# Layer norm applied behind the down projection, with the bounds, the last latents and the weight loads reordered

## The reference

```python
def _layernorm(x):
    return (x - mean(x)) / sqrt(var(x) + 1e-5)

def attn(x):                       # x is the normalised input
    C_q = x @ Wq_d + bq_d          # 1024 -> 12
    C_kv = x @ Wkv_d + bkv_d       # 1024 -> 4
    q = (C_q @ W_qk + b_qk).reshape(b, s, 32, 4)
    attn = softmax(einsum('bqhd,bkd->bhqk', q, C_kv) / sqrt(4))
    V = (C_kv @ Wv_u + bv_u).reshape(b, s, 32, 32)
    return einsum('bhqk,bkhd->bqhd', attn, V).reshape(b, s, 1024) @ Wo + bo

x = x + attn(_layernorm(x))
x = x + ffn(_layernorm(x))         # x @ W.T + bias + sum of eight LoRA products
```

## Time and profile before

| | us |
|---|---|
| three runs | 2119.95, 2121.74, 2122.32 |
| median | 2121.74 |
| the profiled execution | 2122.61 |
| its span, first to last instruction | 2120.8 |
| ACT busy in the span | 1993.5 |
| PE busy in the span | 1958.8 |
| DVE / POOL busy in the span | 504.6 / 180.0 |
| mean granted clock of TensorE | 0.989 |

### The profile page before, as it was taken

One profiled execution on the slowest core, in us unless ns is written; L12 is line 12 of the kernel. 1 busy time (PEld: TensorE's weight loads), 2 busy tenths in 40 slices (PEclk: granted clock), 3 DMA queues, 4 the chain that ended last, 5 costly groups with the idle time before them and its releaser, 6 DMA issues. The chain is left out here.

```text
span 2120.8 us, 35990 instructions
## 1 busy us (share of the span) xinstructions
PE 1958.8 (92%) x15023; PEld 710.0 (33%) x15023; DVE 504.6 (24%) x1307; ACT 1993.5 (94%) x2193; POOL 180.0 (8%) x100
## 2 busy tenths in 40 slices
PE   4757899899999999999999999999999999999999
PEld 3411222233333333333333333333333333333337
DVE  8732343212111111212111111212111111212115
ACT  6968999999999999999999999999999999999970
POOL 1210001000010001100010001100020001100021
PEclk8989999999999999999999999999999999999999
DMA  7541201000010000100010000100010000100010
GB/s 240 184 122 38 84 13 35 5 15 20 18 45 6 25 13 25 35 15 15 24 45 5 25 13 25 35 15 13 25 45 5 22 16 25 35 15 13 25 40 40
DMA packets 45661, 77.42 MB, mean 37 GB/s; under 512 B 15870, under 2 KB 29750, under 8 KB 45498
## 3 DMA queue, kind: packets, MB, share of 16 engines
q1 hardware_dynamic: 45498, 75.11, 10.8%
HBM read 51.23 MB, written 23.86 MB: 35 GB/s over the span
## 5 line engine op out<-in xcount | busy, mean ns | idle before, releaser
L573 ACT ACTIVATE probs<-ps 128x1024 f32<-128x1024 f32 x2048 | 1900.1, 1030 | 34.3 <-PE ps L783 23.8
L794 PE MATMUL ps<-probs,c_wide 128*32 128x512 f32 x8192 | 989.8, 601 | 0.0
L783 PE MATMUL ps<-q_in,key_t 27*128 27x512 bf16 x4096 | 405.1, 386 | 102.9 <-ACT probs L573 91.4
L840 PE MATMUL ps<-w_eff,xn_t 128*128 128x512 f32 x1344 | 394.6, 418 | 0.0
L794 PEld LDWEIGHTS ps<-probs,c_wide 128*32 128x32 f32 x8192 | 212.7, 108 | 426.6 <-issue 221.6
L783 PEld LDWEIGHTS ps<-q_in,key_t 27*128 27x128 bf16 x4096 | 103.0, 91 | 734.7 <-ACT probs L573 714.9
L1263 DVE SCALAR_TENSOR_TENSOR y<-ps,nw,y 128x512 f32<-128x512 f32 x64 | 48.0, 751 | 977.5 <-PE ps L840 967.7
L840 PEld LDWEIGHTS ps<-w_eff,xn_t 128*128 128x128 f32 x1344 | 228.2, 188 | 102.2 <-issue 69.8
L481 POOL TENSOR_TENSOR y<-y,ffn_bias 128x1024 f32<-128x1024 f32 x32 | 76.4, 2387 | 1355.3 <-DVEq L1284 1355.3
L476 POOL TENSOR_TENSOR y<-y,attn_bias 128x1024 f32<-128x1024 f32 x32 | 75.5, 2381 | 481.2 <-DMA y<-in_L_attn_x_dram 481.0
L1247 DVE TENSOR_TENSOR y<-ps,y 128x512 f32<-128x512 f32 x64 | 44.2, 690 | 137.5 <-PE ps L817 137.1
(11 more groups left out here) (136 smaller groups left out, 593.8 us busy)
## 6 DMA issues: line engine op xcount, KB each, us to landing
y<-in_L_attn_x_dram SPq DMA_DIRECT2D x48, 512.0 KB, 4.2
out_dram<-y SPq DMA_DIRECT2D x32, 512.0 KB, 2.7
area<-in_L_attn_x_dram SPq DMA_DIRECT2D x16, 512.0 KB, 4.9
q_in<-q_parts SPq DMA_DIRECT2D x256, 27.0 KB
q_parts<-q_parts_sb SPq DMA_DIRECT2D x48, 128.0 KB, 2.2
y<-in_L_attn_Wo_dram SPq DMA_DIRECT2D x1, 2048.0 KB, 8.5
xn<-in_L_attn_Wo_dram SPq DMA_DIRECT2D x1, 2048.0 KB, 13.5
y<-in_L_ffn_W_dram SPq DMA_DIRECT2D x1, 2048.0 KB, 7.7
```

What stands on the lines that cost most here:

```text
L573: nc.scalar.activation(probs[:, (c * STEPS + step) % PROBS, bass.ts(pair, 2 * N)], ps[:, 2 * (i % SCORE_SLOTS):2 * (i % SCORE_SLOTS) + 2, ...
L783: last = nc.tensor.matmul(ps[:, at, :], key_t[TILE * h:TILE * h + KEYS, bass.ts(b * KT + kt, P)], q_in[TILE * h:TILE * h + KEYS, g % 2, :] ...
L794: last = nc.tensor.matmul(ps[32 * h:32 * h + 32, SUMS, :], c_wide[:, b * KT + kt, at:at + 32], probs[:, (c * STEPS + step) % PROBS, bass.t ...
L840: last = nc.tensor.matmul(ps[:, SHARED, :], xn_t[:, t % 2, a, kb, :], w_eff[:, b, kb, bass.ts(half, N)], start=(kb + i == 0), stop=(kb == ...
```

## The change

The first layer norm is no longer applied to x. PE transposes x as it is loaded. From w_down its column mean is taken off (PE sums the columns with a product with ones, DVE subtracts w_mean), so that the mean of a row drops out, and 1/sqrt of the variance is applied to the down projection: POOL finds it from x_mv (deviations_x, 14 instructions on 128x4), writes it on the diagonal of four 128x128 blocks (diag), PE spreads it over all partitions with a product with ones (spread_r, bank 5), ACT moves that into o_sb (move_r), and DVE multiplies the partial sums by it (scale_parts). x has a ring of four buffers. The biases are added behind, as before.

The first bound is made in bank 6, at kb 2 of the last chunk, and its weights a chunk earlier; DVE splits latents and scales parts inside split_shift(0). For the last latents DVE takes the largest first, ACT reads q_abs first, and the decision is made on the largest of the bound straight from PSUM; the negation stands behind it. SP loads the second group of q_in right behind the first, and the loads of Wv, LoRA B and Wo stand ahead of the last stores and of the decision.

The diff, cut to its core:

```diff
-            def first_tiles(half):
+            def load_tiles(c):
+                if c >= RING:
+                    sp.wait_ge(t_ready, START + (c - RING + 1) * KB)
+                    sp.wait_ge(x_measured, c - RING + 1)
...
                 for t in range(TT):
-                    sp.dma_start(x_tiles[half][:, t, :], x_t[half * TT + t]).then_inc(x_in[half][t], 16)
+                    sp.dma_start(x_tiles[c % RING][:, t, :], x_t[c * TT + t]).then_inc(x_in[c % RING][t], 16)
...
+            load_tiles(1)
...
-            def load_tiles(c, half):
-                for t in range(TT):
-                    sp.wait_ge(xn_ready, c * TT + t + 1)
-                    sp.dma_start(x_tiles[half][:, t, :], x_t[(c + 2) * TT + t]).then_inc(x_in[half][t], 16)
+            load_tiles(2)
+            load_tiles(3)
...
-            for half in range(2):
-                load_tiles(half, half)
-            for i in range(1, CHUNKS // 2 - 1):
-                for half in range(2):
-                    load_tiles(i * 2 + half, half)
-                    store_q(i * 2 + half - 2, half)
+            load_tiles(RING)
+            load_tiles(RING + 1)
+            store_q(0, 0)
+            load_tiles(RING + 2)
+            store_q(1, 1)
+            load_tiles(RING + 3)
+            for c in range(2, CHUNKS - 4):
+                store_q(c, c % 2)
...
             load_q(0, 0, 0, q_loaded[0])
+            load_q(0, 1, 1, q_loaded[1])
             store_shifts(0, 1, CB)
+            sp.wait_ge(t_ready, START + CHUNKS * KB)
+            sp.wait_ge(x_measured, CHUNKS)
+            sp.dma_start(wv_in, wv_u).then_inc(lora_in, 16)
+            for a in range(KB):
+                sp.dma_start(lora_b_sb[:, a], lora_b[:, a * P:(a + 1) * P, :].rearrange("n o r -> o n r")
+                             ).then_inc(lora_in, 16)
+            for half in range(2):
+                sp.dma_start(w_stage[half][:, :, :].rearrange("p t (a n) -> p (t a) n", n=N),
+                             wo[:, half * N:(half + 1) * N].rearrange("(a p) n -> p a n", p=P)).then_inc(stage_in[half], 16)
             for c in (CHUNKS - 2, CHUNKS - 1):
                 store_q(c, c % 2)
             sp.wait_ge(shift_split, 2)
...
+            def deviations_x(c):
+                pool.wait_ge(x_measured, c + 1)
+                pool.tensor_scalar(v, x_mv[:, slot, :, 1], EPS, None, ALU.add).then_inc(p_r, 1)
+                pool.tensor_scalar(r.bitcast(I32), v.bitcast(I32), -0.5, float(0x5F3759DF), ALU.mult, ALU.add).then_inc(p_r, 1)
+                for i in range(3):
+                    pool.tensor_tensor(a, r, r, ALU.mult).then_inc(p_r, 1)
+                    pool.tensor_tensor(a, a, v, ALU.mult).then_inc(p_r, 1)
+                    pool.tensor_scalar(a, a, -0.5, 1.5, ALU.mult, ALU.add).then_inc(p_r, 1)
+                    pool.tensor_tensor(r, a, r, ALU.mult).then_inc(p_r, 1)
+                if c:
+                    pool.wait_ge(r_ps, c)
+                pool.tensor_tensor(diag[:, :, :], ident[:, :].unsqueeze(1).to_broadcast([P, TT, P]),
+                                   r.unsqueeze(2).to_broadcast([P, TT, P]), ALU.mult).then_inc(diag_ready, 1)
...
+            for c in range(CHUNKS):
+                deviations_x(c)
+                if c >= 2:
+                    split_q(c - 2)
+            for c in (CHUNKS - 2, CHUNKS - 1):
+                split_q(c)
...
-            def normalise(c, slot, t):
-                if t == 0:
-                    act.wait_ge(norm_ready, c + 1)
-                nc.scalar.activation(xn_tiles[slot][:, t, :], x_tiles[slot][:, t, :], ACT.Identity,
-                                     bias=nw[:, slot, 2, t:t + 1], scale=nw[:, slot, 3, t:t + 1]).then_inc(xn_ready, 1)
...
+                if c == CHUNKS - 1:
+                    nc.scalar.activation(q_abs[:, c, :], ps[:, 7, :], ACT.Abs, bias=bqk_sb[:, 1:2], scale=SCALE
+                                         ).then_inc(q_read, 1)
...
-            def move_parts(c):
-                act.wait_ge(spread_ps, START + c)
-                act.wait_ge(q_ps, START + c)
-                act.wait_ge(down_done, (c + 2) * KB)
-                nc.scalar.activation(down_part[:, :], ps[:, 4, :], ACT.Copy).then_inc(part_ready, 1)
...
+            def move_r(c):
+                act.wait_ge(r_ps, c + 1)
+                act.wait_ge(part_ready, START + c)
+                nc.scalar.activation(o_sb[:, :], ps[:, 5, :], ACT.Copy).then_inc(r_moved, 1)
...
-            pe.wait_ge(w_in, W_IN)
-            pe.wait_ge(down_ok, 1)
...
+            def first_weights():
+                pe.wait_ge(w_in, W_IN)
+                pe.wait_ge(down_ok, 1)
...
+                last = nc.tensor.matmul(ps[:, 7, 32:32 + KB * 32], ones[:, :], w_down[:, :, :].rearrange("p k n -> p (k n)"),
+                last.then_inc(bias_ps, 1)
...
+                if c or kb >= 4:
-                    last = nc.tensor.transpose(ps[:, kb % 4, bass.ts(t, P)], xn_tiles[slot][:, t, bass.ts(kb, P)], ident[:, :])
+                    if kb == 0:
+                        pe.wait_ge(x_in[c % RING][t], 16 * (c // RING + 1))
+                    last = nc.tensor.transpose(ps[:, kb % 4, bass.ts(t, P)], x_tiles[c % RING][:, t, bass.ts(kb, P)], ident[:, :])
...
+                if c == 0 and four == 0:
+                    pe.wait_ge(down_ok, 4)
...
+            def spread_r(c):
+                nc.tensor.matmul(ps[:, 5, :], ones[:, :], diag[:, :, :].rearrange("p t n -> p (t n)"), start=True, stop=True
...
                 for kb in range(KB):
-                    turn_x(c, slot, kb)
-                    if kb == 1 and not first:
+                    turn_x(c, kb)
+                    if kb == 3 and c == 0:
+                        first_weights()
+                    if kb == 0 and c:
+                        spread_r(c - 1)
+                    if kb == 1 and c:
                         down(c - 1, 1)
+                    if kb == 2 and c == CHUNKS - 2:
+                        pe.wait_ge(caug_ready, START + c - 1)
+                        largest(0, 6)
+                    if kb == 2 and c == CHUNKS - 1:
+                        pe.wait_ge(caug_ready, START + c - 1)
+                        bounds(0, 6)
+                    if kb == 3 and c:
+                        sum_parts(c - 1)
                     if kb == 5:
                         down(c, 0)
-                    if kb == 3 and not first:
-                        if beside is bounds:
-                            pe.wait_ge(bound_w_ready, 1)
-                        sum_parts(c - 1)
-                    if kb == 6 and not first:
-                        use_latents(c - 1, 1 - slot)
-                if beside:
-                    beside(0)
...
+            spread_r(CHUNKS - 1)
...
-                ch.then(nc.vector.tensor_scalar(shift, ps[0:rows, bank, :], -1.0, None, ALU.mult))
-                if smallest is not None:
-                    ch.then(nc.vector.tensor_reduce(smallest, shift, AX.X, ALU.min))
+                if largest is not None:
+                    ch.then(nc.vector.tensor_reduce(largest, ps[0:rows, bank, :], AX.X, ALU.max))
                 if then:
                     then()
+                ch.then(nc.vector.tensor_scalar(shift, ps[0:rows, bank, :], -1.0, None, ALU.mult))
+                dve.sem_inc(bound_read, 1)
+                if then:
+                    dve.wait_ge(first_shift, SHIFT_BLOCKS * 16)
+                    dve.wait_ge(shift_stored, SHIFTS_0)
                 ch.then(nc.vector.tensor_copy(parts[:, 0, :], shift))
                 ch.then(nc.vector.tensor_tensor(rest, shift, parts[:, 0, :], ALU.subtract))
+                if beside:
+                    beside()
...
-                deviations(ch, half)
-                nc.vector.scalar_tensor_tensor(out=nw[:, half, 2, :], in0=mv[:, :, 0], scalar=-1.0, in1=nw[:, half, 3, :],
-                                               op0=ALU.mult, op1=ALU.mult).then_inc(norm_ready, 1)
...
+                ch.wait()
+                if c >= 2:
+                    dve.wait_ge(diag_ready, c - 1)
+                for t in range(TT):
+                    ch.put(nc.vector.bn_aggr(x_mv[:, c % 2, t, :], stats[:, t, :, :].rearrange("p n s -> p (n s)")))
+                ch.end()
+                dve.sem_inc(x_measured, 1)
...
+            def scale_parts(c):
+                nc.vector.tensor_tensor(down_part[:, :], ps[:, 4, :], o_sb[:, :], ALU.mult).then_inc(part_ready, 1)
...
                 if meanwhile:
+                    ch.then(nc.vector.tensor_reduce(c_max[:, bass.ds(c, 1)], src, AX.X, ALU.max, apply_absolute_value=True))
                     meanwhile()
+                    ch.then(nc.vector.tensor_copy(part_b[:, 0, :], src))
...
+            nc.vector.scalar_tensor_tensor(out=w_down[:, :, :], in0=w_mean[:, :].unsqueeze(1).to_broadcast([P, KB, 32]),
+                                           scalar=-1.0 / D, in1=w_down[:, :, :], op0=ALU.mult, op1=ALU.add).then_inc(down_ok, 1)
...
-            statistics(1, 1)
```

(36 more changed lines are left out.)

196 lines of the change are left out of this document (107 added, 89 removed).

## The result

The kernel after takes 2105.07 us, median of four runs (2103.96 to 2106.0); the kernel before, measured beside it, 2121.56 us (2119.95 to 2122.32). The ratio is 0.9924, 95% interval 0.9911 to 0.9936: faster by 0.8%, 16.5 us. The forecast was 2105 us, from a gain of 17.7 us on the profiled execution of before. The profiled execution took 2106.0 us, with a span of 2104.2 against 2120.8 before. The total was right and several of its terms were not, and that is what this part is about.

A forecast was written before the change was run, and what follows sets the result against it. ACT's exponentials were taken as the bound, so only their start and holes could move: 7.0 + 4.6 + 1.9 + 4.2 = 17.7 us off the profiled 2122.6 gave 2104.9, stated as 2105 us, range 2098 to 2113.

The forecast's parts named there:

- What bounds the kernel: ACT's exponentials, 1900.1 us busy of 2120.8, stay unchanged; only their start and the holes after it can move.
- Part 1, the pace: Stage 1 rounds without normalised x: DVE paces at 10.6 us against ACT's 11.3 before; 4.6 us gained.
- PE's round 9.6: TensorE's summed work per stage 1 chunk, 9.6 us, taken as lower bound of DVE's 10.6 us round.
- POOL: GpSimd in stage 1: 14 small instructions at 0.2 us plus 4.3, 7.1 us a round, below DVE's.
- rival D: POOL becomes stage 1's bound: slower by over 0.2% from 0.71 us a small instruction, 2151 at 1 us; chance 0.04.
- Part 2, the start: Start of stage 1: first multiply at 29.8 us instead of 36.80, 7.0 us earlier.
- Rival E: Start: w_in late, or second half, gains lost in the cold clock; gives 4 not 7, 2108; chance within forecast's 0.58.
- T7: End of stage 1's last transposes: forecast at 99.4 us against 110.98 before, 11.6 us gained.
- Part 3, the tail: From the last transposes' end to the decision: 13.1 us instead of 15.0, gain 1.9.
- The 5.9 us behind it stay: From the start of the decision's last instruction to the first exponential: 5.9 us, taken as unchanged.
- Part 4: Second q_in group issued before the weights: ACT's holes of 2.32 and 1.89 us go, gain 4.2.
- the cover of SP's issues: SP's queue after the decision: through some 43 us after the last transposes, beside_attention's first load due at 48, covered.

The follow-up runs named there:

- c1: Kernel after with GpSimd's split of the queries done on one of 512 columns from the third chunk on (part of the computation left out): 2102.99 us, ratio 0.9925.
- h1: Kernel after with VectorE's statistics one chunk ahead, chunk 5's split behind multiply 6, two of ScalarE's query-product copies behind its deviations copy: 2097.66 us, ratio 0.9891.
- e1: Kernel after with 41 spare transposes of the identity put into TensorE's waits behind the last chunk: 2101.33 us, ratio 0.9915.
- f1: Kernel after with 203 do-nothing instructions executed on TensorE, 103 ahead of the first transposes and 100 behind the first chunk: 2109.09 us, ratio 0.9943.
- g1: Kernel after with the last chunk's absolute values taken last of three again and the bound negated before the decision: 2104.9 us, ratio 0.9923.
- f3: Kernel after with 203 do-nothing instructions at the end of TensorE's fallback body, never executed: 2107.3 us, ratio 0.9941.

## Why the prediction came out right, step by step

**What bounds the kernel**: right. The exponentials did not change (1899.9 us), and all of the gain is in their start and in the holes.

**Part 1, the pace**: the size was close, the reason not. I took VectorE as the pace, 9.3 us and 1.3 for held instructions, against TensorE's 9.6. The rounds are 10.15. The hold is real but half as large (0.7 us in the cast alone; the steps with two SBUF inputs at 57.41 ran in 0.75 us like before, and GpSimd's small instructions beside them stretched to 0.72). It is not needed for the round: c1 took it away and the round stayed. The step that failed is "PE's round 9.6" as the lower bound: it added TensorE's work and left out that the sum of parts waits for a multiply, which waits for a copy, which stands behind the copies of the query product on ScalarE. That loop is 10.15 us; with it opened h1 has 9.7 on average, VectorE's own work. VectorE, with 0.7 us of holds in place of 1.3, is level with the loop in after, so my pace was not far off either, and only half of the reason. What I set beside it from the Trainium skill, page "SBUF — State Buffer", section "Who interferes with whom", is borne out in that a cast is held while GpSimd's 128x512 instruction runs, and in that the multiply from PSUM never was (0.69 us in every one); after's steps with two SBUF inputs were held in the tail (111.45, 1.53 us) and not in the rounds.

**POOL**: 0.20 us for a small instruction, as taken, but one every 0.28 us, so the chain takes 3.9 us at the start and not 2.8. Beside VectorE's split some of them stretch, the chain takes 5.0 us, and the round's work is 7.8 us and not 7.1. Below the pace in any case; rival D is far off.

**Part 2, the start**: forecast 29.8, measured 31.23 us. The chain up to statistics(1) is within 0.2 us (18.96 against 19.1). Most of the 1.4 us is a wait of 0.96 for a tile of x, with the DMA engines at a share of 1.03 from 25 to 35 us, and 0.3 in the statistics behind it. The interval behind it was the worse miss: 9.7 forecast, 12.3 measured. I had written that PE's first chunk is done by then, and not asked what an idle TensorE does to the next one. It idled 6.71 us and ran its sum of parts in 2.08 us. Rival E, in its second half, is what happened, and at a larger size than the 4 us left that it had: the start gave 5.6 us, and 2.6 of them went in the cold interval. The four rounds, 10.15 for 10.6, gave 1.8 back and the stretch from multiply 6 to T7 another 1.6 (6.1 us for 7.7), the round ahead of that took 0.3, and T7 came to 10.7 us of gain where 11.6 was forecast.

**Part 3, the tail**: forecast 1.9 us, measured 0.3. The order of steps came out as walked through, but with TensorE at its upper clock in my figures, taken from rows of before, and at the lower one in after: e1 shows 1.8 us for just that, and f1, which kept the upper clock with the same tail, took 13.0 us from T7 to the decision where 13.1 was forecast and after took 14.6. So the step that failed here is the clock that the figures stood on, and it was given no term. g1 shows that two of the steps were worth up to 1.5.

**"The 5.9 us behind it stay"**: wrong, 2.2. I had shown that row and taken the time between decision and first exponential as one fixed thing, without asking what in it was 4 us long. It was one record of the sequencer. f1 to f3 show that it hangs on how many instructions stand ahead of a jump and in the body that it skips, which this change altered by accident.

**Part 4**: 4.2 us as forecast by the holes of before, and the cover of SP's issues held. That this wait would have swallowed most of what is saved between the decision and the first exponential was not foreseen.

**The sum**: -0.9 at T7, -1.6 in the tail, +3.7 at the jump, -1.7 in the gaps right behind the first exponentials, 0 for q_in: together -0.5 against the forecast of 17.7, and that sum is in the ledger's 17.2. A hit by offsetting errors. Without the jump's accident the time would have been near f3's 2107.3, inside the range still.

## What to carry to other kernels

When several engines are near the pace, adding each one's work gives a lower bound only: follow one loop of who releases whom through all of them (here 10.15 us, with 9.07, 7.05 and 9.40 us of work), and look for a copy that is ready early and stands behind others in its queue. A saving that makes TensorE wait can cost its clock behind the wait, as 6.71 us of idling did here and 1.96 us did in some kernels and not in others. So ask of each new idle stretch on TensorE what runs next, and try filling it if that is on the path. And look at the sequencer's own records around every jump before calling a stretch fixed: its price can be 0.4 or 4 us for the same code, and a wait further on may be hiding it.

## What the runs showed of the hardware

TensorE's jump over the fallback took 362, 463, 3534, 3645 and 4052 ns in five kernels that differ, for this purpose, in how many instructions stand ahead of it or in the body; the jumps of ScalarE, SP and VectorE at the same decision took 45 to 72 ns in after. GpSimd needs 0.20 us for an elementwise instruction on 128x4 and starts a dependent one 0.28 us after the start of the one before; on one column a step of its split took 0.19 us, against 1.16 on 512. TensorE's transposes of a spare 128x128 tile, 0.12 us each, kept its granted clock at 1.00 to 112 us in e1, in a tail in which it was 0.50 to 0.60 in after; f1 had 1.00 there without them. And a satisfied double wait on TensorE was not free: 100 of them kept it from its next transposes for 8.4 us in f1.
